# Attention and routing stage of a mixture-of-experts block: double-buffered context, x by groups, late output stores, scalings on ScalarE, unnormalised last routers, sort keys in PSUM

## The reference

```python
x = x + attention(layernorm(x), ctx, ctx)      # one head, 16 sequences of 256 rows, width 256
x = x + ffn(layernorm(x))
# ffn, on all 4096 rows: 8 experts, each takes its 1024 best rows (expert choice)
S = sigmoid(xt @ Wg).T;  G, I = top_k(S, 1024);  ex = xt[I]
hid = gelu(einsum('ekh,ehf->ekf', ex, W1) + b1)          # 256 -> 1024
out = (einsum('ekf,efh->ekh', hid, W2) + b2) * G         # 1024 -> 256
new_x = zeros.at[I].add(out)                             # scatter-add
```

## Time and profile before

| | us |
|---|---|
| median of three runs | 569.58 (568.53 to 570.82) |
| the profiled execution | 573.77 |
| its span, first to last instruction | 571.90 |
| PE busy | 498.6 (87% of the span) |
| DVE busy | 349.2 (61%) |
| ACT busy | 303.8 (53%) |
| POOL busy | 297.3 (52%) |

### The profile page before, as it was taken

The page is one execution under the profiler, slowest core; times in us unless marked ns, Lnnn a source line. Parts: engine busy times, 40 slices in busy tenths (PEclk is TensorE's granted clock), DMA queues, the critical chain, the costliest instruction groups (busy, mean ns, idle before and its releaser), DMA issues.

```text
span 571.9 us, 10360 instructions
## 1 busy us (share of the span) xinstructions
PE 498.6 (87%) x3667; PEld 354.5 (62%) x3667; DVE 349.2 (61%) x759; ACT 303.8 (53%) x544; POOL 297.3 (52%) x431
## 2 busy tenths in 40 slices
PE   4599898898633339999999999999999999999995
PEld 4378587676531124586487487487487487487484
DVE  4468888887678863754754753753753853842721
ACT  3556555444723304925934934943943943953931
POOL 2435988797460041673564564474465365366045
PEclk9989899898855556999999999999999999999998
DMA  8952444554351012494484385385385376274024
GB/s 212 309 198 76 107 112 107 146 130 120 93 142 51 0 44 70 131 176 66 132 166 75 119 159 92 111 151 107 108 145 116 101 144 124 85 157 56 0 29 47
DMA packets 92343, 64.57 MB, mean 113 GB/s; under 512 B 53076, under 2 KB 88216, under 8 KB 92312
## 3 DMA queue, kind: packets, MB, share of 16 engines
q1 hardware_dynamic: 79664, 46.82, 30.9%
q0 software_dynamic: 12288, 17.05, 18.3%
q10 hardware_dynamic: 360, 0.30, 0.2%
HBM read 36.22 MB, written 16.91 MB: 93 GB/s over the span
## 4 chain that ended last, share of the span: by engine, by line
PE 59%; POOL 12%; DVE 7%; issue 7%; SPq 6%; DMA 6%; ACT 3%; POOLq 0%; DVEq 0%; ACTq 0%
PE bank L980 54%; SPq L260 6%; POOL xn L366 3%; DMA rows_d<-xrow 3%; PE bank L1185 3%; POOL xrow L359 2%; POOL out L456 2%; DVE junk L754 2%; DMA ctx<-in_ctx 1%; POOL xrow L357 1%; ACT xn L483 1%; DVE kint L787 1%; DMA out<-yo,ids_s 1%; POOL ex L443 1%; PE bank L1118 1%
## 5 line engine op out<-in xcount | busy, mean ns | idle before, releaser
L980 PE MATMUL bank<-w2h,xres 128*128 128x256 f16 x1024 | 169.0, 273 | 0.0
L980 PE MATMUL bank<-exT,w1h 128*128 128x512 f16 x512 | 154.7, 384 | 0.6 <-DVE exT L966 0.6
L980 PE MATMUL bank<-w2l,xres 128*128 128x256 f16 x512 | 139.6, 273 | 0.0
L925 DVE TENSOR_TENSOR xres<-g,xres 128x512 f16<-128x512 f32 x128 | 87.6, 690 | 62.5 <-ACT xres L592 62.5
L456 POOL DMA_INDIRECT out<-yo,ids_s x64 | 101.4, 1584 | 25.8 <-issue 25.2
L980 PEld LDWEIGHTS bank<-w2h,xres 128*128 128x128 f16 x1024 | 100.2, 98 | 12.5
L588 ACT ACTIVATE g<-bank,b1e 128x512 f32<-128x512 f32 x128 | 88.1, 688 | 27.2 <-PE bank L980 22.3
L980 PE MATMUL bank<-exT,w1l 128*128 128x512 f16 x256 | 98.3, 384 | 0.0
L605 ACT ACTIVATE yo<-yt,ge 128x256 f32<-128x256 f32 x64 | 32.6, 509 | 119.5 <-DVE yt L939 119.5
L980 PEld LDWEIGHTS bank<-exT,w1h 128*128 128x128 f16 x512 | 50.2, 99 | 60.4 <-issue 3.0
L592 ACT ACTIVATE xres<-bank,b1e 128x512 f16<-128x512 f32 x128 | 87.3, 682 | 0.0
(11 more groups left out here) (201 smaller groups left out, 813.9 us busy)
## 6 DMA issues: line engine op xcount, KB each, us to landing
w1r<-in_L_ffn_W SPq DMA_DIRECT2D x8, 1024.0 KB, 6.7
w2r<-in_L_ffn_W SPq DMA_DIRECT2D x8, 1024.0 KB, 5.7
ctx<-in_ctx SPq DMA_DIRECT2D x8, 512.0 KB, 5.5
out<-xres SPq DMA_DIRECT2D x8, 512.0 KB, 4.5
rows_d<-xrow SPq DMA_DIRECT2D x8, 512.0 KB, 3.2
xres<-in_x SPq DMA_DIRECT2D x1, 3072.0 KB, 15.7
xres<-in_x SPq DMA_DIRECT2D x2, 512.0 KB, 8.7
b_bc<-in_L_ffn_b SPq DMA_DIRECT2D x8, 128.0 KB, 3.6
```

The lines of the kernel that those rows point to most:

```text
L925: dve.tensor_tensor(hid[1][:, f, h * 512:(h + 1) * 512], g32[:, u % 2, :], hid[0][:, f, h * 512:(h + 1) * 512], ALU.subtract).then_inc(s[" ...
L980: last = pe.matmul(out, lhs(a, c), rhs(b, c), start=i == 0, stop=i == len(terms) - 1)
```

## The change

- `ctx` becomes two buffers; the loads of context and x of group n+2 are issued together in SP's body n. The one 3 MB load of x is gone.
- SP's body no longer stores `xres`. All of it is stored after the gate store, in four DMAs of 1 MB, followed by the eight loads of `b2`; the first experts' weights are loaded in bodies 6 and 7 instead of 1.
- The bias of the softmax is computed on ACT (with log(PS*QS) in it, so that `rinvs` on DVE goes away: the row sum already holds QS; the high and low halves of p are scaled back).
- `xn2` is no longer an input of the last two routers: raw x is transposed (`x1_transposes`), multiplied by `wgc` (gate weights less their column mean) and the logits are scaled by the reciprocal deviation (`late_logit`). In body 7 PE scores before it attends; v of group 7 goes in two halves.
- The keys and `kint` live in PSUM; ACT writes the keys twice. The second `kint` is computed in the last but one of the eight high rounds.
- In the prologue v and the x transposes of group 0 come ahead of g; the constants of POOL and DVE move to the front, `iota16` behind the first `ln1_scale`.
- The low half of expert 0's W1 is made after the first one-hots instead of in body 8; `next_w1(1)` follows `rows_T(0)`; the split of the last two groups' rows is cut into tiles.

The diff, cut to its core:

```diff
 # SyncE
+            for i in range(2):
+                sp.dma_start(ctx[:, i], cv[:, i * TP:(i + 1) * TP, :]).then_inc(LD_C[i], 16)
+                sp.dma_start(xres[:, i * TP:(i + 1) * TP, :], xv[:, i * TP:(i + 1) * TP, :]).then_inc(LD_X[i], 16)
+            sp.dma_start(bv_bc[:], bv_d.partition_broadcast(P)).then_inc(s["ld_bv"], 16)
             def body(n, k):
-                if runs(n, k, -1):
+                if n + 2 < NP:
                     sp.wait_ge(s["c_tr"], n + 1)
-                    sp.dma_start(ctx[:, :, :], cv[:, tiles(n + 1), :]).then_inc(s["ld_ctx"], 16)
-                if k == 0:
-                    sp.dma_start(xres[:, 2 * TP:NT, :], xv[:, 2 * TP:NT, :]).then_inc(s["ld_x2"], 16)
+                    sp.dma_start(ctx[:, n % 2], cv[:, tiles(n + 2), :]).then_inc(LD_C[n % 2], 16)
+                    sp.wait_ge(s["ln1_st"], 2 * (n + 1))
+                    sp.dma_start(xres[:, tiles(n + 2), :], xv[:, tiles(n + 2), :]).then_inc(LD_X[n % 2], 16)
...
-                if runs(n, k, 1):
-                    sp.wait_ge(s["o_ev"], TP * n)
-                    sp.dma_start(ov[:, tiles(n - 1), :], xres[:, tiles(n - 1), :]).then_inc(s["st_x1"], 16)
             phase_a(body)
             sp.wait_ge(s["gate_r"], 1)
             sp.dma_start(rv[:, :, D:D + E], gate[:, :, :]).then_inc(s["st_gate"], 16)
+            sp.wait_ge(s["o_ev"], TP * NP)
+            for i in range(ST_X1):
+                sp.dma_start(ov[...quarter i...], xres[...quarter i...]).then_inc(s["st_x1"], 16)
+            for e in range(E):
+                sp.dma_start(b2_bc[:, e, :], b2_d[e, :].partition_broadcast(P)).then_inc(s["ld_b2"], 16)
-            next_w1(1)
             rows_T(0, True)
+            next_w1(1)
 # GpSimd
             ln1_scale(0)
+            pool.iota(iota16[:], [[1, P], [0, NT]], base=0, channel_multiplier=0, ...)
+            ln1_scale(1)
+                    for t in range(TP):     # split_rows of groups 6 and 7, the low halves alike
+                        pool.tensor_copy(xrow[:, t, 0, :], xn2[:, m % 2, t]).then_inc(s["row_hi"], 1)
 # ScalarE
-                    for t in range(TP):
-                        if t % 2 == 0:
-                            act.wait_ge(s["s_nb"], 2 * n + t // 2 + 1)
+                    for h in range(2):
+                        act.wait_ge(s["s_max"], 2 * n + h + 1)
+                        act.activation(nbias[:, 2 * h:2 * h + 2], nmax[:, 2 * h:2 * h + 2], ACT.Identity, bias=lift[:], scale=SCORE).then_inc(s["s_nb"], 1)
...
             act.wait_ge(s["key_tr"], 1)
+            act.activation(B_[:, 1, 0:2 * P], A_[:, 0, 0:2 * P], ACT.Sigmoid, scale=1.0 / (XS * AS)).then_inc(s["key_ev"], 1)
             act.activation(keyT[:], A_[:, 0, 0:2 * P]..., ACT.Sigmoid, scale=1.0 / (XS * AS)).then_inc(s["key_ev"], 1)
 # VectorE
-                        dve.tensor_scalar(nbias[:, tl], nmax[:, tl], SCORE, math.log(PS), ALU.mult, ALU.add).then_inc(s["s_nb"], 1)
-                    dve.tensor_scalar(rinvs[:], rinv[:], 1.0 / QS, None, ALU.mult).then_inc(s["s_ris"], 1)
+                def late_logit(m):
+                    dve.wait_ge(s["l_mm"], m + 1)
+                    dve.scalar_tensor_tensor(logit[:, tiles(m), :], src..., AS, rstd2L[:, i]...broadcast_to([P, TP, E]), ALU.mult, ALU.mult).then_inc(s["l_ev"], 1)
+            kb = B_[:, 1, 0:2 * P].bitcast(I32)
+            kint = [C_[:, i, 0:2 * P].bitcast(I32) for i in range(2)]
+                    dve.tensor_scalar(kint[1], kb, (1 << LO_BITS) - 1, None, ALU.bitwise_and).then_inc(s["kint_s"], 1)
+            for j in range(3):
+                w1_lo(0, j)
             read_list(0, True)
             ids_of(0, True)
+            w1_lo(0, 3)
 # TensorE
             def body(n, k):
+                if k == 0:
+                    project_v(0)
+                    x_transposes(0)
                 if runs(n, k, 0):
                     project_g(n)
...
+                if n == NP:
+                    x1_transposes(LAST)
                 if 0 <= n - 3 < LAST:
                     router(n - 3)
+                if n == NP - 1:
+                    score(n)
                 if runs(n, k, 1):
                     attend(n)
...
+                if n == NP:
+                    x1_transposes(LAST + 1)
+                    late_router(LAST)
+                    late_router(LAST + 1)
```

More of the change, by code:

```diff
@@ L372, in _ @@
             ln1_scale(0)
-            pool.wait_ge(s["ld_bv"], 16 * TP)
+            pool.iota(iota16[:], [[1, P], [0, NT]], base=0, channel_multiplier=0,
+                      allow_small_or_imprecise_dtypes=True).then_inc(s["const3"], 1)
+            ln1_scale(1)
+            pool.wait_ge(s["ld_bv"], 16)
             add_bv(0)
+            pool.tensor_copy(ident16[:], ident[:]).then_inc(s["ident16_s"], 1)
             def body(n, k):
-                if runs(n, k, -1):
+                if runs(n, k, -1) and k != 0:
                     ln1_scale(n + 1)
@@ L578, in _ @@
             act.activation(act_tick[:], eps[:, 0:1], ACT.Gelu)
+            act.wait_ge(s["ld_w1"], 16)
+            for c in range(DC):
+                w1_hi(0, c)
             def layer1(e, first):
@@ L689, in body, with low_v @@
-                if runs(n, k, -1) and k != 0:
+                def low_v():
+                    if n < NP - 1:
+                        lo(v[1][:, n % 2], D_[:].rearrange("p a (b d) -> p (a b) d", d=D), v[0][:, n % 2], "v_hi", n + 1, "v_lo")
+                    else:
+                        for h in range(2):
+                            lo(v[1][:, n % 2, 2 * h:2 * h + 2], D_[:, h, :].rearrange("p (b d) -> p b d", d=D),
+                               v[0][:, n % 2, 2 * h:2 * h + 2], "v_hi", n + 1 + h, "v_lo")
@@ L1054, in project_v @@
                                  lambda b, d: wsp[b][:, d, :], DC)
-                last.then_inc(s["v_mm"], 1)
+                    if t == TP - 1 or n == NP - 1 and t == 1:
+                        last.then_inc(s["v_mm"], 1)
             def router(m):
@@ L1080, in transpose_ctx @@
             def transpose_ctx(n):
-                pe.wait_ge(s["ld_ctx"], 16 * (n + 2))
-                transposes(B_, ctx, 0, TP).then_inc(s["c_tr"], 1)
+                pe.wait_ge(LD_C[(n + 1) % 2], landed(n + 1))
+                if n:
+                    pe.wait_ge(s["p_lo"], 2 * n)
+                transposes(B_, ctx[:, (n + 1) % 2], 0, TP).then_inc(s["c_tr"], 1)
             def score(n):
@@ L1136, in body @@
                     transpose_ctx(n)
-                if runs(n, k, 0):
+                if runs(n, k, 0) and n < NP - 1:
                     score(n)
@@ L1140, in body @@
                     transpose_x(n)
-                if k >= NP:
-                    late_router(n - 2)
+                if k == 0:
+                    pe.wait_ge(s["ld_wg"], 16)
+                    pe.wait_ge(s["const1"], 6)
+                    for d in range(DC):
+                        last = pe.matmul(A_[:, 1, 0:E], onesf[:], wg[:, d, :], start=d == 0, stop=d == DC - 1)
+                    last.then_inc(s["u_mm"], 1)
+                if n == NP:
+                    x1_transposes(LAST + 1)
+                    late_router(LAST)
+                    late_router(LAST + 1)
             phase_a(body)
```

382 lines of the change are left out of this document (199 added, 183 removed).

## The result

The changed kernel takes 548.46 us (median of 4 runs, 547.41 to 549.17) beside 570.20 for the kernel before (4 runs, 568.53 to 571.04): ratio 0.9592, 95% interval 0.9543 to 0.9641. 548 was forecast, in a range of 541 to 559. A second set of 6 runs gave 547.31 beside 571.98, ratio 0.9565 [0.9535, 0.9596]. The profiled execution took 549.17, its span 547.4.

The account below looks back on a forecast made before the run. No engine was full over the attention stage; waits for `nbias` and context stretched its loop. 5.75 + 6.9 - 1.5 + 2.0 + 5.2 + 5.1 - 0.8 - 1.0 = 21.65 us saved, median 569.58 to 548; range 541 to 559.

Parts of the forecast that it names:

- four large terms: Savings forecast: prologue 5.75 us, loop 6.9 less 1.5, last logits 5.2, first count 5.1.
- The loop: Attention iterations 1 to 6: period 14.4 us allowed by three engines; 6.9 saved over five periods, 1.5 given back.
- its two stalls: Attention loop: context load late in SP's queue (PE idle 1.98 us); DVE's `nbias` waiting for POOL (3.56 us at worst).
- The prologue: Start to second row maxima: new order brings first maxima at 25.9, second at 40.8 instead of 46.55; 5.75 us saved.
- The tail: Group 6's row maxima to first count: 2.0 us saved to last float16 router, 5.2 to last logits, 5.1 to count.
- Search: First count to first gather: 0.8 us lost to the second integer key and its cast, 1.0 to collisions with POOL.
- The collisions: Search rounds: DVE's threshold updates wait for POOL's split of group 7's rows; 1.0 us lost, between 0 and 3.2.
- Experts: Stage after the first gather: nothing changes, 365.8 us stays within 1 us.
- (1): Loop keeps its 15.8 us period because x or transposed rows land late; 5.4 us lost, 553.5; chance 0.15.
- (2): PE bounds the loop and its clock dips: 15.05 us a period, late products at half clock; 551; chance 0.13.
- (4): Output stores and b2 in one queue land too late for expert 0's copies; 573, 3 us slower; chance 0.04.
- (3): Prologue fails: iota16 or a late x of group 1 holds ACT; 5.75 us lost, 554; chance 0.08.

Follow-up runs that it names:

- the second profile: The changed kernel run once more, unchanged: 547.31 us, ratio 0.9565 to the kernel before.
- The experiment with the iota: Changed kernel with the 4.2 us `iota16` moved back behind the row split of the last groups: 548.48 us, ratio 0.9597 to the kernel before.
- the kernel with both edits: Kernel before plus softmax bias on ACT and SP's part (two context buffers, x by groups, stores behind the gate store): 567.95 us, ratio 0.9964.

## Why the prediction was right

The mechanisms of the four large terms hold; the sum of 21.65 became 24.5 in the profile, 21.7 between the medians of the first set and 24.7 between those of the second.

That the median came within 0.5 us of 548 is in part luck. The forecast took 4.2 us off the profile's figure, because the profiled execution of before lay that far above its median; that of the changed kernel lay 0.7 above its own, and took 549.17 where 552.1 was forecast. Inside, a prologue 1.6 short stands against 1.8 in the experts that nobody forecast, 1.1 in the search, 0.8 in the loop and 0.8 in the tail. The first count "near 146" came at 145.97 only with the late start of that execution; in the second profile it is at 142.16.

- **The loop.** "6.9 saved, and I give back 1.5" makes 5.4; it gave 6.23. Too much was given back: periods of 14.56 at clock 1.00 are 0.16 over the 14.4 that three engines allow, 0.66 over five periods (the first was 14.42). The experiments add what the prediction did not see: its two stalls hide each other. Alone their edits are worth 2.4 and 0.8 us of loop and no median that stands out from no change, together 6.0 (0.36% of the median, in an interval that just leaves out 0).
- **The prologue.** 5.75 forecast, 4.12 in the first profile. The chain holds for the usual execution and is up to 1.6 us slow there (first maxima 25.9 forecast, 24.31 to 25.75 in six of eight; second at 38.7 to 40.1, a saving of 6.5 to 7.9); left out was that PE may hold its lower level over the first 18 us. The experiment that undid the order alone cost 0.6 to 0.9% (0.9656 against 0.9592 and 0.9565), but its interval overlaps both of theirs.
- **The tail.** Router 1.81 for 2.0, logits 5.82 for 5.2, first count 5.42 for 5.1. "So POOL and SP, not attention, set this point" is borne out by the kernel without maxima. The late product set at 3.42 took 2.72. What unnormalised rows are worth depends on the order around them: in the new order going back to normalised rows costs 9.7 us of tail (40.59 - 30.88), more than the term, because attention then waits behind the statistics too.
- **Search.** 1.8 lost forecast, 0.68 measured. The round with the second integer key takes 2.32 us from count to count (155.94 to 158.26) where the round with the cast took 1.71: 0.6 for 0.8. The collisions are the mis-sized term, 0.2 for 1.0: POOL's split is over at 149.98, only two updates are struck (0.34 and 0.39 instead of 0.22), and one round takes 1.81 instead of 1.63. The experiment with the iota confirms the mechanism.
- **Experts.** 0 forecast, 1.78 measured, and no run isolates a part of the change in it: over all profiles of both kernels and the variants this stretch takes 363.2 to 365.8 us, and that of before is the longest.
- **The rivals.** None came true: no wait for context or x in the loop (1), clock 1.00 there (2). The output stores leave from 150.97 and b2 is issued by 168.6, and DVE's first copy of gathered rows runs at 189.40 without a wait (4). A late prologue (3) there was, in some executions, but not by iota16, which ends at 18.63: the second deviations are out at 20.56, the normalised x that needs them runs at 23.94.

Open stays what unnormalised rows alone would bring in the old order, and whether a quicker chain of row split, store and transposes would let a faster loop through; neither was tried. Open too are the experts' 1.78 us and what holds PE at its lower level in some prologues.

## What to carry to other kernels

Two waits in one iteration that end at about the same time should be removed together: alone the edits gave 2.4 and 0.8 us of loop here, both 6.0. Before a loop is shortened further, ask what the work behind it waits for: 6 us taken out of this loop came back as 7 us of tail. Judge a prologue by several profiles (one was 3.8 us off), and compare a profile with its own set of times first: those of before and of the kernel with both edits lay on opposite sides of their medians.

## What was not expected of the hardware

- The clock of a window can read 1.00 while PE works at its lower level: 0 to 28.08 has 1.00, though products of 128x256 take 0.42 us each until 18.33 and 0.27 from 18.49 on. The trace's first clock record begins at 18.4 us, and a window counts what no record covers as full speed.
- A scaling of two columns, 0.17 us by itself, cost 5.5 us over five periods when put back on DVE, because it lasts until POOL's addition ends.
- Integer conversions of 128x256 took 0.43 and 0.42 us out of PSUM, 0.29 each between SBUF tensors.
